# Attention scores of four row groups in four PSUM banks at once, with the round's order rewritten

## Time and profile before

| what | us |
|---|---|
| median of 3 runs (802.25 to 809.67) | 803.47 |
| the profiled execution, in all | 801.58 |
| its span (first to last instruction) | 799.9 |
| attention stage, to the first expert product | 348.0 |
| expert stage | 451.9 |

### The profile page before, as it was taken

How to read it: one execution, slowest core, us unless ns; L and a number is a source line. 1 busy time by engine, 2 the same in 40 slices (tenths; PEclk the granted TensorE clock), 3 DMA queues, 4 the chain that set the end, 5 groups by cost and what they waited for, 6 DMA issues and landing times.

```text
span 799.9 us, 19528 instructions
## 1 busy us (share of the span) xinstructions
PE 749.2 (94%) x6592; PEld 675.1 (84%) x6593; DVE 500.8 (63%) x1162; ACT 395.2 (49%) x909; POOL 322.2 (40%) x357
## 2 busy tenths in 40 slices
PE   5899999999999999679999999999999999999993
PEld 4667777777777767469999999999999999999993
DVE  5576867777676876836465565665665655656642
ACT  3336263635353534525465465554564655655542
POOL 3001010000000212025666666666666666666663
PEclk9999999999999999879999999999999999999997
DMA  2420303030303122154354363453463543633332
GB/s 82 131 81 1 107 0 106 0 106 0 106 0 106 14 82 25 54 163 103 60 120 80 60 141 59 95 103 67 83 114 59 111 90 60 136 63 58 62 59 34
DMA packets 51860, 59.58 MB, mean 74 GB/s; under 512 B 9344, under 2 KB 48256, under 8 KB 51840
## 3 DMA queue, kind: packets, MB, share of 16 engines
q0 software_dynamic: 19776, 27.16, 21.2%
q1 hardware_dynamic: 32064, 32.16, 13.4%
HBM read 37.15 MB, written 22.15 MB: 74 GB/s over the span
## 4 chain that ended last, share of the span: by engine, by line
PE 71%; DVE 15%; issue 6%; ACT 4%; DMA 1%; SPq 1%; DVEq 0%; POOL 0%; ACTq 0%; POOLq 0%
PE A L1074 13%; PE A L1075 12%; PE A L1076 12%; PE O L1074 6%; PE O L1075 6%; PE O L1076 6%; PE S L1114 3%; DVE s_sb L765 3%; PE S L1076 3%; PE S L1075 3%; PE S L1074 3%; PE A L1306 3%; PE O L1141 1%; DVE xT_lo L742 1%; ACT oh_rhs L531 1%
## 5 line engine op out<-in xcount | busy, mean ns | idle before, releaser
L456 POOL DMA_INDIRECT out<-ybuf,s_idx x98 | 161.5, 1648 | 62.7 <-POOL s_idx L452 44.7
L1074 PE MATMUL A<-gT_hi,w_hi 128*128 128x256 f32 x588 | 165.1, 281 | 1.6 <-DVE gT_lo L1018 1.6
L1075 PE MATMUL A<-gT_lo,w_hi 128*128 128x256 f32 x588 | 164.8, 280 | 0.0
L1076 PE MATMUL A<-gT_hi,w_lo 128*128 128x256 f32 x588 | 164.6, 280 | 0.0
L440 POOL DMA_INDIRECT xg<-gather_table,g_idx x100 | 100.4, 1004 | 94.2 <-issue 63.7
L368 POOL TENSOR_TENSOR on_lo<-on,on_hi 128x512 fp32r<-128x512 f32 x15 | 19.2, 1279 | 294.2 <-ACT on_hi L517 294.2
L1049 DVE TENSOR_TENSOR h_lo<-h,h_hi 128x256 fp32r<-128x256 f32 x196 | 83.6, 426 | 79.5 <-ACT h_hi L693 79.4
L1074 PE MATMUL O<-w_hi,h_hi 128*128 128x256 f32 x392 | 114.4, 292 | 2.0 <-DVE h_lo L1049 2.0
L693 ACT ACTIVATE h_hi<-h 128x256 fp32r<-128x256 f32 x196 | 82.0, 418 | 65.3 <-DVE h L1045 57.4
L1074 PEld LDWEIGHTS A<-gT_hi,w_hi 128*128 128x128 f32 x588 | 112.5, 191 | 2.0 <-issue 2.0
L1075 PEld LDWEIGHTS A<-gT_lo,w_hi 128*128 128x128 f32 x588 | 111.4, 189 | 0.0
(11 more groups left out here) (182 smaller groups left out, 1575.1 us busy)
## 6 DMA issues: line engine op xcount, KB each, us to landing
w_raw<-wffn SPq DMA_DIRECT2D x72, 192.0 KB, 3.0
xa<-x SPq DMA_DIRECT2D x8, 512.0 KB, 5.9
gather_table<-xna SPq DMA_DIRECT2D x8, 512.0 KB, 4.6
xr<-x SPq DMA_DIRECT2D x8, 512.0 KB, 5.8
out<-yout SPq DMA_DIRECT2D x8, 512.0 KB, 3.1
out<-ybuf,s_idx POOLq DMA_INDIRECT x104, 3.9
xg<-gather_table,g_idx POOLq DMA_INDIRECT x100
w_raw<-wqk_nat SPq DMA_DIRECT2D x1, 512.0 KB, 5.3
```

Source lines behind the costliest of these rows:

```text
L456: pool.indirect_dma_start(out=out, out_offset=bass.IndirectOffsetOnAxis(ap=s_idx[:, sub:sub + 1], axis=0), in_=ybuf[:, sub, :], in_offset= ...
L1074: mm(out_ap, l_hi, r_hi, start=(k == 0), stop=False)
L1075: mm(out_ap, l_hi, r_lo, start=False, stop=False)
L1076: return mm(out_ap, l_lo, r_hi, start=False, stop=(k == n - 1))
```

## The change

The PSUM banks are named anew. A ring of three banks holds O[0], A[2] and O[1], and the scores of all four row groups of a quad (`scores(s, quad)`, four times a block) go to four banks at once: the two S banks and two of the ring. DVE still makes two evictions of 128x1024 for a quad, one from each pair of banks, with a four-dimensional access pattern. The mean squares move to the S banks, most other users of the A banks change place, and `proj_ps` now counts each projection (8 a block where it was 4). All five programs are one `round_of` for each block in place of two halves: on TensorE the four `values` come in two pairs, the output projection stands between scores 2 and 3, and one-hot products and ranks near the end; DVE starts a round with the next block's statistics, and has the eight evictions in pairs. SyncE stores the normalized tokens and loads the next block ahead of the router's weights. In the last round the order is its own, and the first half's head norm moves behind the expert weights' split. In the beginning the order of the four fused matrices is f = 3, 2, 1, 0 (keys first), the low parts of the keys' come before those of the tokens, TensorE waits for each matrix when it uses it, twelve matmuls on the identity run first (`WARM`), and GpSimd clears `idx_acc` and `vz` only after the first block's statistics are done (`xstat_ok`).

The diff, cut to its core (of the rewritten lists the new ones stand, which replace `first_half` and `second_half` above):

```diff
-        A = [ps(f"A{i}", [P, 512]) for i in range(4)]
+        ring = ps("ring", [P, 3, 512])
+        A = [ps("A0", [P, 512]), ps("A1", [P, 512]), ring[:, 1, :], ps("A3", [P, 512])]
         S_both = ps("S", [P, 2, 512])
         S = [S_both[:, i, :] for i in range(2)]
-        k_banks = [(A[0], A[2]), (A[3], A[0])]
-        q_banks = [(A[1], A[3]), (A[2], A[1])]
-        values_banks = [A[0], A[1], A[2], A[3]]
-        kt_banks = [A[0], A[3]]
-        wo_banks = [A[2], A[1]]
-        rank_bank = idx_bank = A[0]
-        ms_bank = A[1]
-        xt_banks = [A[2], A[0]]
-        O = [ps(f"O{i}", [P, 512]) for i in range(2)]
+        O = [ring[:, 0, :], ring[:, 2, :]]
+        score_banks = [(S_both[:, :, :], ring[:, 0:2, :]), (S_both[:, :, :], ring[:, 0:3:2, :]),
+                       (S_both[:, :, :], ring[:, 1:3, :]), (S_both[:, :, :], ring[:, 1:3, :])]
+        ring_first = (1, 1, 0, 1)
+        k_banks = [(A[3], A[0]), (A[0], A[3])]
+        q_banks = [(A[1], A[2]), (A[1], A[2])]
+        values_banks = [A[0], A[1], A[3], A[3]]
+        kt_banks = [A[0], A[1]]
+        wo_banks = [A[3], A[0]]
+        last_wo_banks = [A[2], A[1]]
+        rank_bank, last_rank_bank = A[2], A[1]
+        idx_bank, last_idx_bank = A[1], A[3]
+        ms_banks = S
+        xt_banks = [A[3], A[0]]
+        fused_order = [(3, A[0]), (2, A[3]), (1, A[2]), (0, A[1])]
...
             g.memset(base[:, :, :], 0.0)
+            g.memset(yout[:, 0, 0:1], 0.0).then_inc(yout_free, DMA)
+            pool.wait_ge(xstat_ok, 1)
             g.memset(idx_acc[:, :, :, :], 0.0)
             g.memset(vz[:, :, :, :, :], 0.0).then_inc(counts, 1)
-            g.memset(yout[:, 0, 0:1], 0.0).then_inc(yout_free, DMA)
...
+            def round_of(s, first, last):
+                queries_masked(s, 0)
                 values_out(s, 0)
                 values_out(s, 2)
+                values_out(s, 1)
+                if not last:
+                    token_rstd(s + 1)
                 if not first:
                     heads_hi(s - 1, 1)
                 values_out(s, 3)
                 keys_by_token(s, 0)
+                queries2(s, 1)
                 act.wait_ge(ls_ok, s + 1)
                 a.activation(ex[:, :, :], ls[:, :, :], ACT.Exp).then_inc(ex_ok, 1)
                 if not last:
+                    norm_apply(s + 1)
+                if last:
                     one_hot_tokens(s - 1)
                 keys2(s, 1)
                 queries_masked(s, 1)
+                if not first and not last:
+                    one_hot_tokens(s - 1)
+                squares(s, 0)
                 keys_by_token(s, 1)
                 if not last:
                     front(s + 1)
                 if last:
                     one_hot_tokens(s)
+                    return
+                squares(s, 1)
                 head_rstd(s, 0)
+                keys2(s + 1, 0)
                 heads_hi(s, 0)
+                head_rstd(s, 1)
+                queries2(s + 1, 0)
...
+            def fused_hi(i):
+                f, bank = fused_order[i]
+                act.wait_ge(fused_ps, i + 1)
+                a.activation(wqk_hi[:, f, :, :].rearrange("p c n -> p (c n)"), bank[:, :], ACT.Copy).then_inc(setup_act, 1)
+            fused_hi(0)
+            fused_hi(1)
+            front(0, S)
+            fused_hi(2)
+            fused_hi(3)
...
+            head_rstd(NBLK - 1, 0)
             head_rstd(NBLK - 1, 1)
+            heads_hi(NBLK - 1, 0)
             heads_hi(NBLK - 1, 1)
...
             def masked_scores(s, p):
+                quad, b = p // 2, p % 2
+                banks = score_banks[quad][b ^ ring_first[quad]]
                 dve.wait_ge(s_ps, 2 * NPAIR * s + 2 * p + 2)
-                v.tensor_tensor(s_sb[:, 2 * p % NS:2 * p % NS + 2, :, :].rearrange("p a n c -> p (a n) c"),
-                                S_both[:, :, :].rearrange("p a (n c) -> p (a n) c", n=4),
-                                causal[:, :].unsqueeze(1).to_broadcast([P, 8, P]), ALU.mult).then_inc(s_ok, 1)
+                v.tensor_tensor(s_sb[:, 2 * p % NS:2 * p % NS + 2, :, :],
+                                banks.rearrange("p a (n c) -> p a n c", n=4),
+                                causal[:, :].unsqueeze(1).unsqueeze(1).to_broadcast([P, 2, 4, P]), ALU.mult).then_inc(s_ok, 1)
...
+            def round_of(s, first, last, chain):
+                if not last:
+                    norm_stats(s + 1, chain)
+                if last:
+                    one_hot(s - 1, 0)
                 logits_out(s, 0)
                 masked_scores(s, 0)
+                masked_scores(s, 1)
                 logits_out(s, 1)
+                if not last:
+                    norm_refine(s + 1, chain)
                 softmax_head(s, chain)
                 state(s, 0)
                 queries(s, 1)
+                if last:
+                    one_hot(s - 1, 1)
+                masked_scores(s, 2)
+                masked_scores(s, 3)
+                softmax_tail(s, chain)
+                keys(s, 1)
                 choose(s, 0, chain)
                 choose(s, 1, chain)
+                if last:
+                    add_indices(s - 1)
                 choose(s, 2, chain, first)
+                if last:
+                    masked_scores(s, 4)
+                    slots(s, 0, chain, last_rank_bank)
+                    masked_scores(s, 5)
+                    slots(s, 1, chain)
+                    add_residual(s - 1, 0)
+                    one_hot(s, 0)
+                    one_hot(s, 1)
+                    masked_scores(s, 6)
+                    state(s, 1)
+                    add_residual(s - 1, 1)
+                    masked_scores(s, 7)
+                    return
+                if not first:
+                    one_hot(s - 1, 0)
                 masked_scores(s, 4)
+                masked_scores(s, 5)
                 if not first:
                     add_residual(s - 1, 0)
                     add_residual(s - 1, 1)
+                    one_hot(s - 1, 1)
+                masked_scores(s, 6)
                 state(s, 1)
+                masked_scores(s, 7)
+                for c in range(KC):
+                    tokens_low(s + 1, c)
                 if not first:
                     add_indices(s - 1)
+                slots(s, 0, chain)
+                slots(s, 1, chain)
                 head_norm(s, 0, chain)
+                keys(s + 1, 0)
+                head_norm(s, 1, chain)
+                queries(s + 1, 0)
...
+            head_norm(NBLK - 1, 0, chain)
             head_norm(NBLK - 1, 1, chain)
             outputs_low(NBLK - 1, 1)
             for i in range(2):
-                add_residual(NBLK - 1, i)
+                add_residual(NBLK - 1, i, last_wo_banks)
...
+            def scores(s, quad, first=False):
+                half, chunk = quad // 2, quad % 2
+                if quad == 2:
                     pe.wait_ge(qk_ok, 4 * s + 4)
+                if chunk == 0:
                     pe.wait_ge(qz_ok, 2 * s + half + 1)
+                if quad == 0 and not first:
+                    pe.wait_ge(on_ok, 2 * s - 1)
+                    pe.wait_ge(ln_o_ok, 2 * s)
+                if quad == 1 and not first:
+                    pe.wait_ge(on_ok, 2 * s)
+                if quad:
+                    pe.wait_ge(s_ok, NPAIR * s + 2 * quad)
                 for n in range(2):
                     t = n * 2 + chunk
                     tok = slice(t * P, (t + 1) * P)
+                    for g in range(PAIRS):
                         rows = slice(32 * g, 32 * g + 32)
+                        bank = score_banks[quad][(g // 2) ^ ring_first[quad]][:, g % 2, :]
+                        last = mm(bank[:, n * 2 * P:(n + 1) * 2 * P], k[rows, half, tok], qz[rows, half, :, tok],
                                   start=True, stop=True, tile_position=(32 * g, 0))
                         if n == 1:
                             last.then_inc(s_ps, 1)
...
-                pe.wait_ge(s_ok, NPAIR * s + 2 * (quad + 1))
+                pe.wait_ge(s_ok, NPAIR * s + 2 * (quad + 1) + (1 if chunk == 0 else 0))
...
+            def round_of(s, first, last):
                 pe.wait_ge(qk_ok, 4 * s + 1)
...
                 values_logits(s, 0)
                 values_logits(s, 2)
                 pe.wait_ge(qk_ok, 4 * s + 2)
+                values_logits(s, 1)
                 scores(s, 0, first)
+                pe.wait_ge(lg_ok, 2 * s + 1)
+                values_logits(s, 3)
+                keys_by_token(s, 0)
+                pe.wait_ge(s_ok, NPAIR * s + 1)
+                project(q_banks[1][1], 1, 1).then_inc(proj_ps, 1)
+                pe.wait_ge(lg_ok, 2 * s + 2)
+                project(q_banks[1][0], 0, 1).then_inc(proj_ps, 1)
+                state(s, 0)
+                scores(s, 1, first)
+                project(k_banks[1][1], 3, 1).then_inc(proj_ps, 1)
+                pe.wait_ge(kv_ok, 2 * s + 1)
+                project(k_banks[1][0], 2, 1).then_inc(proj_ps, 1)
```

(113 more changed lines are left out.)

186 lines of the change are left out of this document (44 added, 142 removed).

## The result

The changed kernel takes 772.53 us (median of 4 runs, 770.52 to 773.3) where the kernel before takes 802.86 beside it: 0.96 of the time, 95% interval 0.9545 to 0.9656. That is 30 us less, against the 35.8 of the forecast. The profiled execution took 772.14 us, with a span of 770.5.

A forecast was written before the change was run, and what follows sets the result against it. TensorE's own work was taken to bound a round, until DVE's list stands in front. Savings 3.7 + 4.9 + 23.4 + 3.8 = 35.8 us took the median from 803.5 to 767.7, said as 768; own range 761 to 775, 760 to 784 with rival 1.

The forecast's parts named there:

- The failed step: Moves counted as free: next block's statistics ahead of `logits_out` on DVE, about 2 us; SyncE's stores and loads within a round.
- the term for the first round: First round: 32.3 us against 37.2, a floor of 29.1 plus stalls of 3.0 at scores 3 and 0.2 before; saved 4.9.
- Rival 3: Slower: the masked eviction on DVE becomes longer, at 0.7 us more rounds of 40.9 and 813 us in all; chance 0.05.
- Scores and width: Scores on TensorE: four row groups at once cost 1.06 us a quad, saving 4.24 a round; work falls from 37.3 to 33.1.
- rival 2: Scores on TensorE: four row groups don't run at once; 38.3 us a round, 793 us in all; chance 0.09.
- Stalls: TensorE's waits for DVE in each round: 0.2 us after scores 0, 1.1 at scores 3, 0.8 at values 2; 2.1 together.
- The six rounds: The six rounds after the first: 35.3 us each against 39.19, ends 33.1 and 37.4; 23.4 us saved.
- Rival 1: DVE's order is worse than laid out: twice the stalls, rounds of 37.4 us, 784 us in all; chance 0.14.
- Beginning: Before the first scores: low parts 2.4 us, `var_eps` 0.6 and order of the maps 0.7; 3.7 saved, ends 0 and 5.
- the order of the maps: Beginning: the factor with the second map is projected first, so ACT's copy runs beside the other projection; 0.7 us saved.
- Last round: Last block: last eviction ends 28.1 us after first scores, 4.1 saved, less 0.3 for the moved head norm; net 3.8.
- Evictions and the expert stage: DVE's eight evictions still take 1.22 us each, and the expert stage behind the rounds is unchanged.

The follow-up runs named there:

- e2: The changed kernel, with SyncE storing the first normalized tokens and loading the second block before the first expert's weight pieces; 761.3 us.
- e1: The changed kernel with heads of row groups 2 and 3 computed on row groups 0 and 1, at most two at once; 786.4 us.
- e3: The changed kernel with each eviction masking only the first half of its columns from the second block on; 759.31 us.
- e8: The changed kernel with both at most two row groups at once and half-masked evictions from the second block on; 784.36 us, a single run.
- e9: The changed kernel with the second block's load early and both halves of the one-hot rows moved from in front of masks on DVE; 755.0 us.
- e6: The changed kernel with GpSimd's two memsets not waiting for the first statistics; 770.25 us, a single run.
- e7: The changed kernel with TensorE waiting for all four factor matrices before the first projection; 769.91 us, a single run.
- e5: The changed kernel without the twelve warm-up matmuls (WARM = 0); 771.52 us, a single run.
- e4: The changed kernel with the second block's load early and the second half of the one-hot rows behind a block's last eviction; 758.09 us.
- e10: The changed kernel with the second block's load early and only the first half of the one-hot rows moved, ahead of the first state update; 756.38 us.
- e12: The changed kernel with the second block's load early, no warm-up, memsets early and TensorE waiting for all four factor matrices; 764.65 us.

## Why the prediction was right, and which of its steps failed

The time, 772.5, lies inside the forecast's own range (761 to 775), by a sum with one wrong sign in it and one error the other way.

**The failed step** is this: "`norm_stats` now stands in front of `logits_out` on DVE, about 2 us in the time in which `qz` is made", with "SyncE's stores and loads move within a round that uses them a round later". Both hold in the six rounds. In the first round the data of `norm_stats` are not there: SyncE's eight weight pieces stand in front of their load, and all eight were in the trace of before. I looked at the cost of the moved work on DVE, not at when its input lands. In place of 4.9 saved, 6.1 were lost: 11.0 off. The runs put 10.2 of it on the load (43.28 to 33.07 in e2): 8.54 are TensorE's wait, and nearly all the rest is the lower clock of the work right behind it. With the load early the term for the first round comes out, 33.07 against 32.3, with a stall at scores 3 of 2.1 where I had 3.0. Rival 3 named a longer eviction as the way to lose; the loss that came was a wait that no rival had.

**Scores and width: right.** 1.08 a quad against 1.06; 1.92 at two row groups, so rival 2 falls. The Trainium skill ("TensorE: Matmul & The Clock Gate", Measured speedup vs the span model), with its 3.07 times, gave 1.12 by an estimate; 16 x 0.215 / 1.08 is 3.2, so the trace nearly agrees. Width and the four ends saved are 8 x 1.06 − 4 x 1.08 = 4.2 us, as forecast. But the 37.3 from which I took them was misread: the window of the earlier trace rows runs to 330 us, 33 us into the last round. Over the six whole rounds it is 225.90 / 6 = 37.65, with 1.5 idle and not 1.9:

```profile
62.30:297.40 235.10, 225.90 (x2126) 171.65 (x2126) 174.73 (x426) 108.82 (x217) 19.52 (x17) 1.00 0.18 53
```

So TensorE's work fell by 37.65 − 32.87 = 4.8. The 0.6 more is mainly what the ends of the mean squares saved, net of the projections (above), which I had at nothing. That work came out at 32.87 for 33.1 is two errors of mine that nearly cancel. Matmul ends are modelled, and some records may be missing, in both numbers.

**Stalls: right in kind and nearly in sum**, 1.55 against 2.1, at the places named; but scores 3 had 0.33 where I had 1.1, and `qz` 0.23 where I had 0.1. The six rounds saved 28.7 where I had 23.4; of the 0.9 that a round is under its forecast (35.3 − 34.4), 0.7 is stalls with the last handover (2.2 − 1.5) and 0.2 TensorE's work.

**That the masks give back half of the width**, 1.7 of 3.4 us, was in the forecast as stalls, and e1, e3 and e8 show it. The Trainium skill ("TensorEngine Tiling (Array Packing)", PSUM Bottleneck) warns that emptying PSUM may become the limit once TensorE is faster; here it took half of the width's gain, not all, and e9 took back 1.06 of the 1.7 by order alone (34.43 to 33.37). Rival 1 (twice the stalls) did not come.

**Beginning: right in sum, and of no worth that these runs show.** 3.5 against 3.7; `var_eps` 0.17 against 1.03, and the moved memsets gave 0.72 in e6 where I had 0.6. Waiting for each matrix gave 1.26 (e7), a part of the 2.4 for the low parts; no run takes the order of the maps, costed at 0.7, by itself. The warm-up, costed at nothing, gives 0.31 at the first projection. But e5 to e7 take back between 0.3 and 1.3 us there and lose no time in their single runs, as the load is behind them.

**Last round: 3.0 against 3.8.** The last eviction ended 27.8 us after the first scores (forecast 28.1); from there to the output projection it took 10.6 and not 9.5. DVE and ACT in the timeline of the kernel after:

```profile
297.91 1.21 DVE L778 TENSOR_TENSOR s_sb<-S,causal 128x1024 f32<-128x1024 f32 x1
...
302.46 0.60 ACT L585 ACTIVATE sq<-ring 128x512 f32<-128x512 f32 x1 [5.24 <-PE ring L1168]
...
304.61 0.68 ACT L515 ACTIVATE ln_o<-S,eps 128x512 f32<-128x512 f32 x1
...
307.21 0.69 DVE L864 TENSOR_TENSOR on<-ring,rstd_o 128x512 f32<-128x512 f32 x1 [0.55 <-ACT rstd_o L517]
308.60 0.99 DVE L859 TENSOR_TENSOR on_lo<-on,on_hi 128x512 fp32r<-128x512 f32 x1 [0.69 <-ACT on_hi L522]
```

The moved head norm has two passes on ACT (`ln_o`, `rstd_o`) that now stand ahead of the second half's: from the first `ln_o` to the projection it took 5.13 us, where before it took 3.92. My sum had 0.3 for the moved norm. From the end of the last eviction to `sq` it took 3.34 us, little more than the 3.06 before. But the chain of waits runs through TensorE there: with 0.50 of the clock from 296.08 to 300.96, the products with the values that `sq` waits for took 1.87 and 1.48 us where the rounds have 1.08 and 1.01.

**Evictions and the expert stage: unchanged**, as costed (1219 and 1214 ns; 0.87 of the clock against 0.85). Rival 3 falls.

## What to carry to other kernels

When an instruction moves to the head of an engine's list, follow its input back to the DMA that brings it, round by round and the first one above all: what a load is queued behind costs nothing until somebody waits for it first. When TensorE's work is made shorter, expect part of the gain back as waits for the engine that empties its banks, and look then for work in front of those evictions that could stand behind them. A gain ahead of a wait with a fixed end is no gain until that end is moved.

## What the runs showed of the hardware that I had not expected

- The stretch in which TensorE stood idle for 8.5 us had 0.67 of the clock (a mean of the two levels, 1.2 and 2.4 GHz), and the busy 33 us after it 0.89; with the load early the stretch from 22 to 32 us had 1.00. The work right behind the idle stretch took 1.5 us more for it.
- In the first round of the kernel after and of all that differ from it only in the load, the one-hots or the beginning, TensorE also stands for 2.1 us at scores 3, released by a mask. Right behind that the clock was at its lower level for a while in some and not in others: from 38 to 41 us 0.50 in e2, 0.54 in e4, 0.60 in e9, but 1.00 in e10. From scores 3 to block 1 they took 16.79, 16.98 and 16.90 us against 15.35; e12, e6 and e7 are like e10, the kernel after and e5 like e2. TensorE's program of that round is the same in all; what tells them apart stays open.
- Two row groups more at a time cost nothing: the 16 listed matmuls of a quad took 1.08 us on four groups where 8 had taken 1.06 on two.
